# One more turned chunk per unit, and one chunk fewer on GpSimd, in a two-way state-space scan

## The chip, the cores and the metric

The kernel runs on one core of one Trainium2 chip. The metric is the device time of one execution in microseconds. A core has five engines with queues of their own: TensorE (PE), VectorE (DVE), ScalarE (ACT), GpSimd (POOL) and SyncE (SP), which here only issues DMAs. They meet at semaphores, and each works through its own instructions strictly in the order in which they are written.

## The reference, cut to what matters

There are 4 batches of 1024 tokens with 512 features. Normalisations and projections make, for each batch, `z1` and `z2` (1024 tokens by E = 1024 channels). Each goes through a state-space scan with N = 16 states per channel, the second one backward in time:

```python
dbc = einsum('bse,re->bsr', u, Wdbc)
dlt, Bm, Cm = split(dbc, [R, R + N])
delta = softplus(einsum('bsr,er->bse', dlt, Wdt) + bdt)
dA  = exp(delta[..., None] * A)                       # decay of each state
dBu = delta[..., None] * Bm[:, :, None, :] * u[..., None]   # inflow of each state
h = dA_t * h + dBu_t                                  # over the tokens t
y = einsum('ben,bn->be', h, C_t)                      # sum over the 16 states
# u * Dp is added; y1 and y2 are gated by silu(mx), added, projected by Wf,
# and gate * (projection + bf + skip) is added to x
```

## The kernel before

`setup_kernel` takes the first 0.3 ms or so: conditioning, folded weights, normalised tokens, the rows of B and C in memory. `ssm_kernel`, where the change lies, takes the rest. It is written out, without loops on the chip, as NU = 64 **units** k: batch by batch, 8 tiles of 128 channels forward, then the same 8 backward. A unit lays 128 channels on the partitions and 1024 tokens along them, and goes through 16 **chunks** c, one for each state; q = 16k + c counts chunks through. For each chunk these things happen:

- a decay: ACT takes the exponential of `delta` (line 983);
- an inflow: delta times u times the row B of this state;
- the scan itself on DVE (line 1118), with h as output;
- a product of h with the row C of this state, into one of four buffers `hbuf`;
- a sum: PE adds the product, turned, onto `y` (`sum_chunk`, line 768, 8 transposes), three steps after the scan.

The letters of the string `KINDS` say which engine does the inflow and the product:

- **V**: POOL makes the inflow (`inflow`, line 1019, into one of DR = 3 buffers `dbu`), DVE the product (line 1123).
- **P**: POOL makes both the inflow and the product (`product`, line 1024).
- **A**, a "turned" chunk: ACT scales `dut` (delta times u, turned so that tokens lie on the partitions) by a column of B, in two halves of four instructions (`scale_half`, line 945), PE turns the result back into PSUM (`turn_inflow`, line 779, 8 transposes), and POOL makes only the product.

Where the decay goes differs too. For V and P it goes into PSUM buffer `slot[q % 2]`, which is free when chunk q - 2 has been scanned (and multiplied, if that was a V). For A it goes into the single buffer `dec`, free when the A before it has been scanned; its inflow takes `slot[q % 2]`.

Each engine's order is written by hand, step by step over c. On **ACT** a step is: the decay of chunk c, then whatever the tables put there. `SCALE_STEPS` names the half of which later chunk is scaled at which step. At step 1 the second half of a sigmoid of the unit before follows (`sigmoid_half`, 4 instructions from line 920), at step 2 `copy_y` of the unit before (line 936), at steps 4 and 5 the softplus of the next unit (from line 901), and at step 15 the first half of the sigmoid. On **PE** a step c turns chunk c if it is an A, then sums chunk c - 3, then does matmul pieces for the next unit. On **POOL** a step makes the product of the chunk before (unless a V) and the inflows that `INFLOWS_AT` lists: the inflow of the third pooled chunk on, one step after its buffer is scanned.

Three sorts of units occur, by k mod 16:

- **sigmoid units** (1 to 8; 32 in all): the sigmoid halves and the matmuls `mx_part` behind them are done.
- **result units** (9 to 15 and 0, from k = 16 on; 24): at step 7 PE runs `transpose_y` for the unit before (behind the sum of chunk 4) and DVE gates it (`gate_y`, line 1092). PE projects a block of the batch before, DVE adds to it at step 1 (line 1097), and POOL finishes it (`finish_result`, lines 1030 and 1033) at step 3.
- **gating units** (9 to 15 of the first batch; 7): the same without a result block. Unit 0 has none of these.

Of the kernel before, what the change touches and what calls it, by code (L numbers as in the profile page):

```python
# [27 lines left out]
def setup_kernel(nc, t, scratch):  # L28

    with ExitStack() as ctx:  # L30
# [301 lines left out]
        def _(pe):  # L332
# [88 lines left out]
            for c in range(NC):  # L421
# [2 lines left out]
                project(1, c, ps[c % 2])  # L424


KINDS = "VPVVAVAPAVAPAPAV"
SCALE_STEPS = {0: (4, 0), 2: (4, 1), 3: (6, 0), 5: (6, 1), 6: (8, 0), 7: (8, 1),
               8: (10, 0), 9: (10, 1), 10: (12, 0), 11: (12, 1), 12: (14, 0), 13: (14, 1)}
SEQ = ET * N  # L430
HR = 4
# [5 lines left out]
def kind(q):  # L437


    return KINDS[q % N]  # L440


def before(kinds, q):

    return sum(KINDS.count(x) * (q // N) + KINDS[:q % N].count(x) for x in kinds)

# [13 lines left out]
def ssm_kernel(nc, t, scratch):  # L460

    with ExitStack() as ctx:
# [55 lines left out]
        def half(h):  # L518
            return slice(h * TC, (h + 1) * TC)
# [5 lines left out]
        def has_mx(k):  # L525
            return not gates(k) and k % (2 * ET) != 0
# [364 lines left out]
        def _(act):  # L891
# [46 lines left out]
            def scale_half(q, h):  # L938
                a, g, n = before("A", q), q // SEQ, q % N
                act.wait_ge(dut_ready, 2 * (q // N) + h + 1)  # L940
                act.wait_ge(bt_ready, g + 1)
                if a >= 2:
                    act.wait_ge(turned, a - 1)
                for j in range(TB * h, TB * h + TB):
                    last = nc.scalar.activation(abuf[:, a % 2, j * P:(j + 1) * P], dut[:, j * P:(j + 1) * P],  # L945
                                                ACT.Copy, scale=bt[:, g % 2, j, n:n + 1])
                last.then_inc(scaled, 1)
# [6 lines left out]
            def copy_dut(k, h):  # L954
                act.wait_ge(dut_mm, 2 * k + h + 1)
                if k > 0:
                    act.wait_ge(scaled, len(SCALE_STEPS) * k - 1 + h)
                nc.scalar.activation(dut[:, half(h)], mb[h][:], ACT.Copy).then_inc(dut_ready, 1)
# [9 lines left out]
            for k in range(NU):  # L968
                f, zs = wtile(k), z_step(k)
                new_b = (k + 1) % ET == 0  # L970
                for c in range(N):
# [7 lines left out]
                    else:  # L979
                        if q >= 2:  # L980
# [3 lines left out]
                                         scale=par[:, f // ET, f % ET, PA + c:PA + c + 1]).then_inc(decay_ready, 1)  # L984
                    if c in SCALE_STEPS:
                        scale_half(N * k + SCALE_STEPS[c][0], SCALE_STEPS[c][1])
                    if c == 1 and k > 0 and has_mx(k - 1):
# [220 lines left out]
```

## Time and profile before

| | us |
|---|---|
| median of 3 runs | 3499.4 |
| lowest, highest | 3492.81, 3507.31 |
| the profiled execution | 3504.69 |
| its span | 3502.9 |
| busy in the span: DVE, POOL | 3134.3, 3134.6 |
| busy in the span: PE, ACT | 2926.2, 2628.9 |

The profile holds one execution. A row of a timeline gives the start, the duration, the engine, the line, and what is written from what; in brackets stands how long the engine had been idle before and what ended that. Durations overlap a little, since an instruction's end is still being written while the next begins; so the text often takes the distance from one start to the next.

### The profile page before, as it was taken

Reading aid. Unit: us, or ns where it says so; the run is one execution under the profiler, and the core shown is the slowest. Engines: PE = TensorE matmul, PEld = TensorE weight load, DVE = VectorE, ACT = ScalarE, POOL = GpSimd, SP = SyncE. Lnnn points to the kernel's source line nnn. Section 1 sums busy time; section 2 is a strip of 40 time slices with the busy share of each in tenths; the row PEclk is TensorE's granted clock in tenths of the full one; section 3 lists DMA queues with packets and bytes.
Section 4 is the critical chain, followed back from the end, with each engine's and each line's share of the span. In section 5 each row is a group of like instructions: output and inputs, shape, how many; then the busy total and the mean of one; then the engine's idle time right before and its main releaser. Section 6 shows DMA issues by size and latency. Waiting matters only on the chain.

```text
span 3502.9 us, 47926 instructions
## 1 busy us (share of the span) xinstructions
PE 2926.2 (84%) x16208; PEld 2105.5 (60%) x16208; DVE 3134.3 (89%) x2109; ACT 2628.9 (75%) x5032; POOL 3134.6 (89%) x1418
## 2 busy tenths in 40 slices
PE   8996888887778888888888888888988888888877
PEld 4653656666656666566666666666666666666663
DVE  1853999999999999999999999999999999999970
ACT  0223888888888899887777888987777998887750
POOL 0522999999999999999999999999999999999982
PEclk9987899999899999999999999999999999999998
DMA  5566344654456344645566344645575443655444
GB/s 204 199 206 239 126 144 144 219 185 148 155 185 248 132 152 156 247 152 170 172 232 237 130 143 147 250 167 173 168 260 194 151 149 136 238 174 175 167 137 119
DMA packets 231497, 624.16 MB, mean 178 GB/s; under 512 B 22012, under 2 KB 76476, under 8 KB 227416
## 3 DMA queue, kind: packets, MB, share of 16 engines
q1 hardware_dynamic: 228520, 600.16, 49.8%
q0 software_dynamic: 2592, 18.88, 1.6%
q8 instruction: 129, 2.11, 0.2%
q10 hardware_dynamic: 144, 2.10, 0.2%
q14 instruction: 112, 0.92, 0.1%
HBM read 540.28 MB, written 80.76 MB: 177 GB/s over the span
## 4 chain that ended last, share of the span: by engine, by line
POOL 32%; issue 25%; PE 19%; DVE 14%; ACT 1%; POOLq 0%; DVEq 0%; DMA 0%; SPq 0%; ACTq 0%
POOL dbu L1019 16%; POOL hbuf L1024 15%; DVE hbuf L1118 8%; PE y L768 7%; PE mb L741 6%; DVE slot L1118 4%; PE slot L779 3%; DVE du L1068 1%; PE mb L815 1%; PE mb L818 1%; DVE delta L1058 1%; ACT abuf L945 0%; PE mb L731 0%; POOL skip L1030 0%; POOL xn L1030 0%
## 5 line engine op out<-in xcount | busy, mean ns | idle before, releaser
L1019 POOL TENSOR_TENSOR dbu<-bst,du 128x1024 f32<-128x1024 f32 x640 | 1506.6, 2373 | 37.2 <-DVE du L1068 23.7
L1024 POOL TENSOR_TENSOR hbuf<-hbuf,cres 128x1024 f32<-128x1024 f32 x640 | 1507.9, 2373 | 35.4 <-DVE hbuf L1118 34.1
L768 PE MATMUL y<-ident,hbuf 128*128 128x128 f32 x8192 | 1136.4, 290 | 292.3 <-POOL hbuf L1024 291.9
L768 PEld LDWEIGHTS y<-ident,hbuf 128*128 128x128 f32 x8192 | 1004.9, 150 | 479.3 <-POOL hbuf L1024 382.4
L945 ACT ACTIVATE abuf<-dut,bt 128x128 f32<-128x128 f32 x3072 | 971.0, 387 | 0.0
L1118 DVE TENSOR_TENSOR_SCAN hbuf<-dec,slot 128x1024 f32<-128x1024 f32 x384 | 874.5, 2277 | 38.1 <-PE slot L779 18.2
L1118 DVE TENSOR_TENSOR_SCAN slot<-slot,dbu 128x1024 f32<-128x1024 f32 x384 | 875.6, 2280 | 16.6 <-POOL dbu L1019 15.4
L983 ACT ACTIVATE slot<-delta,par 128x1024 f32<-128x1024 f32 x640 | 710.3, 1110 | 217.6 <-DVE hbuf L1123 204.9
L1118 DVE TENSOR_TENSOR_SCAN hbuf<-slot,dbu 128x1024 f32<-128x1024 f32 x256 | 580.5, 2267 | 1.2 <-ACT slot L983 1.2
L779 PE MATMUL slot<-ident,abuf 128*128 128x128 f32 x3072 | 424.8, 284 | 178.1 <-ACT abuf L945 172.4
L983 ACT ACTIVATE dec<-delta,par 128x1024 f32<-128x1024 f32 x384 | 438.3, 1141 | 153.8 <-DVE hbuf L1118 153.8
L779 PEld LDWEIGHTS slot<-ident,abuf 128*128 128x128 f32 x3072 | 362.6, 146 | 293.9 <-ACT abuf L945 203.7
L741 PE MATMUL mb<-xn,wzs 128*128 128x512 f32 x1024 | 504.6, 617 | 3.7 <-DVE delta L1058 3.7
L1123 DVE TENSOR_TENSOR hbuf<-slot,cres 128x1024 f32<-128x1024 f32 x384 | 470.2, 1224 | 13.2
L741 PEld LDWEIGHTS mb<-xn,wzs 128*128 128x128 f32 x1024 | 184.5, 201 | 140.2 <-issue 140.2
L751 PE MATMUL mb<-xn,wx 128*128 128x512 f32 x512 | 240.9, 593 | 0.0
L828 PE MATMUL mb<-wf,ybuf 128*128 128x512 f32 x448 | 207.7, 609 | 23.9 <-issue 23.9
L731 PE MATMUL mb<-dl,wdt 81*128 81x512 f32 x256 | 138.8, 656 | 47.4 <-DVE skip L1097 20.7
L828 PEld LDWEIGHTS mb<-wf,ybuf 128*128 128x128 f32 x448 | 83.5, 196 | 112.9 <-issue 112.9
L914 ACT ACTIVATE ud<-mb,par 128x512 f32<-128x512 f32 x128 | 98.3, 768 | 45.8 <-PE mb L741 45.8
L393 PE MATMUL ps<-wz,wct 128*128 128x512 f32 x256 | 121.4, 615 | 10.6 <-DMA wct<-in_wcT 10.6
L751 PEld LDWEIGHTS mb<-xn,wx 128*128 128x128 f32 x512 | 87.3, 190 | 61.2 <-issue 61.2
(101 smaller groups left out, 2050.2 us busy)
## 6 DMA issues: line engine op xcount, KB each, us to landing
bst<-bc_s SPq DMA_DIRECT2D x640, 512.0 KB, 4.2
cres<-bc_s SPq DMA_DIRECT2D x128, 512.0 KB, 8.0
wzs<-wz_s SPq DMA_DIRECT2D x64, 256.0 KB
yf_s<-yrd SPq DMA_DIRECT2D x32, 512.0 KB, 5.4
yg_s<-ybuf SPq DMA_DIRECT2D x32, 512.0 KB, 2.9
ybuf<-yf_s SPq DMA_DIRECT2D x31, 512.0 KB, 5.7
si_s<-silu SPq DMA_DIRECT2D x28, 512.0 KB, 6.1
silu<-si_s SPq DMA_DIRECT2D x28, 512.0 KB, 4.5
```

The costliest lines, as they stand in the source:

```text
L731: nc.tensor.matmul(mb[h][:], wdt[:, k % 2, :], dl[:, half(h)], start=True, stop=True).then_inc(dps_mm, 1)
L741: last = nc.tensor.matmul(mb[h][:], wz[:, k % 2, i * P:(i + 1) * P], xn[:, h, i, :], start=(i == 0), stop=(i == DT - 1))
L751: last = nc.tensor.matmul(mb[h][:], wx[:, i * P:(i + 1) * P], xn[:, h, i, :], start=(i == 0), stop=(i == DT - 1))
L768: last = nc.tensor.matmul(y[:, j * P:(j + 1) * P], hbuf[:, q % HR, j * P:(j + 1) * P], ident[:], start=False, stop=(q % N == N - 1), is_tr ...
L779: last = nc.tensor.matmul(slot[q % 2][:, j * P:(j + 1) * P], abuf[:, a % 2, j * P:(j + 1) * P], ident[:], start=True, stop=True, is_transp ...
L828: last = nc.tensor.matmul(bank[:], yp_tile(i)[:, e, :], wf[:, e, :], start=(e == 0), stop=(e == ET - 1))
L945: last = nc.scalar.activation(abuf[:, a % 2, j * P:(j + 1) * P], dut[:, j * P:(j + 1) * P], ACT.Copy, scale=bt[:, g % 2, j, n:n + 1])
L983: nc.scalar.activation(decays, delta[:, k % 2, :], ACT.Exp, scale=par[:, f // ET, f % ET, PA + c:PA + c + 1]).then_inc(decay_ready, 1)
L1019: nc.gpsimd.tensor_tensor(dbu[:, i % DR, :], bst[:, i % BR, :], du[:, k % 2, :], ALU.mult).then_inc(pool_b, 1)
L1024: nc.gpsimd.tensor_tensor(hbuf[:, q % HR, :], hbuf[:, q % HR, :], cres[:, q % N, :], ALU.mult).then_inc(pool_prod, 1)
L1118: nc.vector.tensor_tensor_scan(h[:, ::step], decays[:, ::step], inflows[:, ::step], 0.0, ALU.mult, ALU.add).then_inc(scanned, 1)
L1123: nc.vector.tensor_tensor(hbuf[:, q % HR, :], slot[q % 2][:], cres[:, c, :], ALU.mult).then_inc(dve_prod, 1)
```

## The change

Chunk 2 becomes an A (it was a V), and chunk 11 a V (it was a P). So a unit has 6 V, 3 P and 7 A, where it had 6 V, 4 P and 6 A. `SCALE_STEPS` gets two halves more, those of chunk 2 at steps 0 and 1; the halves of chunks 4 and 6 now stand at steps 2 to 5 (before: 0, 2, 3 and 5).

```diff
-KINDS = "VPVVAVAPAVAPAPAV"
-SCALE_STEPS = {0: (4, 0), 2: (4, 1), 3: (6, 0), 5: (6, 1), 6: (8, 0), 7: (8, 1),
+KINDS = "VPAVAVAPAVAVAPAV"
+SCALE_STEPS = {0: (2, 0), 1: (2, 1), 2: (4, 0), 3: (4, 1), 4: (6, 0), 5: (6, 1), 6: (8, 0), 7: (8, 1),
                8: (10, 0), 9: (10, 1), 10: (12, 0), 11: (12, 1), 12: (14, 0), 13: (14, 1)}
```

ACT's order in a sigmoid unit, from the decay of chunk 2 to that of chunk 5 (L983 is a decay, L945 x4 a scaled half, L936 `copy_y`, L901 and L903 the softplus). Before:

```order
L983 ACTIVATE slot0<-delta,par 128x1024
L945 ACTIVATE abuf<-dut,bt 128x128 x4
L936 ACTIVATE yrd<-y 128x1024
L983 ACTIVATE slot1<-delta,par 128x1024
L945 ACTIVATE abuf<-dut,bt 128x128 x4
L983 ACTIVATE dec<-delta,par 128x1024
L901 ACTIVATE soft<-mb0 128x512
L901 ACTIVATE soft<-mb1 128x512
L903 ACTIVATE soft<-soft 128x1024
L983 ACTIVATE slot1<-delta,par 128x1024
```

ACT, the same place now:

```order
L983 ACTIVATE dec<-delta,par 128x1024
L945 ACTIVATE abuf<-dut,bt 128x128 x4
L936 ACTIVATE yrd<-y 128x1024
L983 ACTIVATE slot1<-delta,par 128x1024
L945 ACTIVATE abuf<-dut,bt 128x128 x4
L983 ACTIVATE dec<-delta,par 128x1024
L945 ACTIVATE abuf<-dut,bt 128x128 x4
L901 ACTIVATE soft<-mb0 128x512
L901 ACTIVATE soft<-mb1 128x512
L903 ACTIVATE soft<-soft 128x1024
L983 ACTIVATE slot1<-delta,par 128x1024
```

The decay of chunk 2 goes to `dec`, and a scaled half stands between the decay of chunk 4 and the softplus; another half stands ahead of this piece, between the decay of chunk 1 and the sigmoid.

POOL's order from the product of chunk 13 to the product of chunk 4 of the next unit (the number in `c_in` is the product's chunk; L1019 is an inflow; in a result unit `finish_result` stands ahead of the last inflow). Before:

```order
L1024 TENSOR_TENSOR hbuf<-hbuf,cres 128x1024 [waits scanned,c_in13]
L1019 TENSOR_TENSOR dbu<-bst,du 128x1024 [waits scanned,du_ready,b_in2]
L1019 TENSOR_TENSOR dbu<-bst,du 128x1024 [waits scanned,du_ready,b_in0]
L1024 TENSOR_TENSOR hbuf<-hbuf,cres 128x1024 [waits scanned,c_in14]
L1019 TENSOR_TENSOR dbu<-bst,du 128x1024 [waits scanned,du_ready,b_in1]
L1019 TENSOR_TENSOR dbu<-bst,du 128x1024 [waits scanned,du_ready,b_in2]
L1024 TENSOR_TENSOR hbuf<-hbuf,cres 128x1024 [waits scanned,c_in1]
L1019 TENSOR_TENSOR dbu<-bst,du 128x1024 [waits scanned,du_ready,b_in0]
L1019 TENSOR_TENSOR dbu<-bst,du 128x1024 [waits scanned,du_ready,b_in1]
L1019 TENSOR_TENSOR dbu<-bst,du 128x1024 [waits scanned,du_ready,b_in2]
L1024 TENSOR_TENSOR hbuf<-hbuf,cres 128x1024 [waits scanned,c_in4]
```

POOL, the same place now:

```order
L1024 TENSOR_TENSOR hbuf<-hbuf,cres 128x1024 [waits scanned,c_in13]
L1019 TENSOR_TENSOR dbu<-bst,du 128x1024 [waits scanned,du_ready,b_in0]
L1019 TENSOR_TENSOR dbu<-bst,du 128x1024 [waits scanned,du_ready,b_in1]
L1024 TENSOR_TENSOR hbuf<-hbuf,cres 128x1024 [waits scanned,c_in14]
L1019 TENSOR_TENSOR dbu<-bst,du 128x1024 [waits scanned,du_ready,b_in2]
L1019 TENSOR_TENSOR dbu<-bst,du 128x1024 [waits scanned,du_ready,b_in0]
L1024 TENSOR_TENSOR hbuf<-hbuf,cres 128x1024 [waits scanned,c_in1]
L1019 TENSOR_TENSOR dbu<-bst,du 128x1024 [waits scanned,du_ready,b_in1]
L1024 TENSOR_TENSOR hbuf<-hbuf,cres 128x1024 [waits scanned,c_in2]
L1019 TENSOR_TENSOR dbu<-bst,du 128x1024 [waits scanned,du_ready,b_in2]
L1024 TENSOR_TENSOR hbuf<-hbuf,cres 128x1024 [waits scanned,c_in4]
```

One inflow has gone from this piece and the product of chunk 2 has come into it, so it is eleven instructions long both times. The instruction that POOL is spared is the product of chunk 11, which stood between those of chunks 10 and 12.

PE, around the start of a unit (L768 is a sum, 8 transposes each; L751 `mx_part`, L779 a turned chunk, L731 a matmul for the next unit's delta). Before:

```order
L751 MATMUL mb<-xn,wx 128x512 x2
L768 MATMUL y<-ident,hbuf 128x128 x8
L751 MATMUL mb<-xn,wx 128x512 x2
L768 MATMUL y<-ident,hbuf 128x128 x16
L731 MATMUL mb<-dl,wdt 128x512 x2
```

PE, the same place now:

```order
L751 MATMUL mb<-xn,wx 128x512 x2
L768 MATMUL y<-ident,hbuf 128x128 x8
L751 MATMUL mb<-xn,wx 128x512 x2
L768 MATMUL y<-ident,hbuf 128x128 x8
L779 MATMUL slot<-ident,abuf 128x128 x8
L768 MATMUL y<-ident,hbuf 128x128 x8
L731 MATMUL mb<-dl,wdt 128x512 x2
```

The turned chunk 2 stands between the sums of chunks 14 and 15 of the unit before.

## Rows read from the trace of the kernel before

**Rows 1.** The page's first part: each engine's busy time and share.

```profile
PE 2926.2 (84%) x16208; PEld 2105.5 (60%) x16208; DVE 3134.3 (89%) x2109; ACT 2628.9 (75%) x5032; POOL 3134.6 (89%) x1418
```

**Rows 2.** Windows: span, busy time (instructions) by engine; units 2-8, 10-14, 26-32.

```profile
core 0: us, PE busy (x) PEld busy (x) DVE busy (x) ACT busy (x) POOL busy (x), PEclk, DMA share, GB/s
422.55:753.75 331.20, 281.27 (x1606) 202.82 (x1605) 324.50 (x198) 298.33 (x569) 325.89 (x141) 0.94 0.50 172
800.68:1033.69 233.01, 177.45 (x1140) 141.76 (x1140) 231.00 (x142) 188.36 (x365) 232.79 (x101) 0.90 0.45 155
1555.26:1902.66 347.40, 292.48 (x1720) 223.43 (x1719) 328.94 (x204) 264.65 (x512) 343.74 (x155) 0.93 0.59 201
```

**Rows 3.** Waits, whole span: who waited for whom, us, times, longest.

```profile
DVE ybuf L1092 <- PE mb L818: 44.0, 32, 2.6
```

**Rows 4.** Timeline of ACT, sigmoid units 20 to 21: decay 15 to decay 5.

```profile
1312.03 1.12 ACT L983 ACTIVATE slot<-delta,par 128x1024 f32<-128x1024 f32 x1 [0.43 <-DVE hbuf L1118]
1315.09 0.69 ACT L920 ACTIVATE soft<-mb,par 128x512 f32<-128x512 f32 x1 [1.94 <-PE mb L751]
...
1317.67 1.10 ACT L983 ACTIVATE slot<-delta,par 128x1024 f32<-128x1024 f32 x1
1318.71 1.26 ACT L945 ACTIVATE abuf<-dut,bt 128x128 f32<-128x128 f32 x4
1319.88 1.10 ACT L983 ACTIVATE slot<-delta,par 128x1024 f32<-128x1024 f32 x1
...
1332.21 1.12 ACT L983 ACTIVATE slot<-delta,par 128x1024 f32<-128x1024 f32 x1 [0.22 <-DVE hbuf L1123]
```

**Rows 5.** Timeline of DVE there: scans 14 and 15, later scan 5, scan 14.

```profile
1312.55 2.29 DVE L1118 TENSOR_TENSOR_SCAN hbuf<-dec,slot 128x1024 f32<-128x1024 f32 x1 [0.55 <-issue]
1314.76 2.27 DVE L1118 TENSOR_TENSOR_SCAN slot<-slot,dbu 128x1024 f32<-128x1024 f32 x1
1317.06 1.23 DVE L1123 TENSOR_TENSOR hbuf<-slot,cres 128x1024 f32<-128x1024 f32 x1
1318.20 0.74 DVE L1078 SCALAR_TENSOR_TENSOR silu<-mb,par,soft 128x512 f32<-128x512 f32 x1
...
1334.29 2.27 DVE L1118 TENSOR_TENSOR_SCAN slot<-slot,dbu 128x1024 f32<-128x1024 f32 x1
...
1359.61 2.29 DVE L1118 TENSOR_TENSOR_SCAN hbuf<-dec,slot 128x1024 f32<-128x1024 f32 x1 [0.55 <-issue]
```

**Rows 6.** Timeline of PE, end of unit 21: sum 10, turn 14, sum 11, `mx_part`.

```profile
1355.40 1.09 PE L768 MATMUL y<-ident,hbuf 128*128 128x128 f32 x8 [1.27 <-POOL hbuf L1024]
...
1358.48 1.04 PE L779 MATMUL slot<-ident,abuf 128*128 128x128 f32 x8
1359.35 1.04 PE L768 MATMUL y<-ident,hbuf 128*128 128x128 f32 x8
1360.23 1.88 PE L751 MATMUL mb<-xn,wx 128*128 128x512 f32 x4
```

**Rows 7.** Timeline of POOL, result units 28 to 29: products 12 and 13, product 4.

```profile
1696.42 4.71 POOL L1024 TENSOR_TENSOR hbuf<-hbuf,cres 128x1024 f32<-128x1024 f32 x2 [0.30 <-DVE hbuf L1118]
...
1724.58 2.36 POOL L1024 TENSOR_TENSOR hbuf<-hbuf,cres 128x1024 f32<-128x1024 f32 x1
```

**Rows 8.** Timeline of PE, result unit 29: the sum of chunk 4.

```profile
1726.99 1.97 PE L768 MATMUL y<-ident,hbuf 128*128 128x128 f32 x8 [3.36 <-POOL hbuf L1024]
```

**Rows 9.** Timeline of DVE, result units 28, 29: gating, scans 8, 13 and 15.

```profile
1680.84 0.69 DVE L1092 TENSOR_TENSOR ybuf<-mb,silu 128x512 f32<-128x512 f32 x1 [1.84 <-PE mb L818]
...
1683.33 2.29 DVE L1118 TENSOR_TENSOR_SCAN hbuf<-dec,slot 128x1024 f32<-128x1024 f32 x1 [0.24 <-PE slot L779]
...
1730.49 1.49 DVE L1092 TENSOR_TENSOR ybuf<-mb,silu 128x512 f32<-128x512 f32 x2 [1.36 <-PE mb L818]
1732.22 2.29 DVE L1118 TENSOR_TENSOR_SCAN hbuf<-dec,slot 128x1024 f32<-128x1024 f32 x1 [0.24 <-PE slot L779]
...
1745.08 2.27 DVE L1118 TENSOR_TENSOR_SCAN hbuf<-slot,dbu 128x1024 f32<-128x1024 f32 x1
...
1750.10 2.27 DVE L1118 TENSOR_TENSOR_SCAN slot<-slot,dbu 128x1024 f32<-128x1024 f32 x1
```

## The prediction

> **What bounds the kernel now.** I read the busy shares first, then windows cut at unit borders, then the waits, then timelines of two places. The page shows DVE and POOL level at 89% [rows 1], which tells nothing of which waits for which, so I went by sorts of units [rows 2]. Seven sigmoid units take 331.2 us, 47.3 each, with DVE busy 324.5 and POOL 325.9; five gating units 46.6 each, DVE and POOL both within 0.5 us of full; seven result units 49.6 each, POOL busy 343.7 of 347.4, but DVE only 328.9, so DVE is idle 2.6 us in each. The waits name where: DVE waits for `transpose_y` at the gating [rows 3].
>
> In a sigmoid unit the reader should see that DVE sets the pace. Scan 14 begins at 1312.55 and again at 1359.61: 47.06 us, of which 0.55 is a wait at scan 14 [rows 5]; DVE's own work is thus 46.5. PE makes that wait: at step 13 its sum had waited 1.27 us for POOL, and the matmuls behind it stood ahead of the turning of chunk 14 [rows 6].
>
> In a result unit I see a loop through three engines. POOL starts products 12 and 13 as soon as scan 12 lets it [0.30 idle, rows 7], works without a pause to product 4 of the next unit, and PE had waited 3.36 us for that product [rows 8]; the sum and the transposes end DVE's wait at the gating, 1.36 us [rows 9]; from there DVE runs to scan 13, and the loop closes. One turn, 1680.84 to 1730.49, is 49.65 us [rows 9].
>
> **The change part by part.** What it removes: one POOL instruction per unit. Product 13 starts near 1696.42 + 2.33 = 1698.75 and product 4 ends at 1726.94, 28.2 us for eleven instructions and a finished block [rows 7]; a POOL instruction is about 2.33 (two products in 4.67, from 1696.42 to 1701.1). So POOL is spared 2.33 x 64 = 149 us. But the one it is spared, product 11, stands outside the stretch from product 13 to product 4, and that stretch keeps eleven instructions. DVE does the same sixteen scans and six products; one product moves from chunk 2 to chunk 11. One broadcast of B fewer per unit leaves SP's queue; none of the waits I read ends on one, so I cost it at nothing.
>
> What it adds: on PE 8 transposes, 0.87 us at the upper clock (1358.48 to 1359.35 [rows 6]), between the sums of chunks 14 and 15; behind them queue sum 15, and behind that `copy_y` on ACT. On ACT two scaled halves, 1.17 each (1318.71 to 1319.88 [rows 4]), 2.34 us per unit.
>
> **Sigmoid units.** Before, ACT's run from the sigmoid at 1315.09 has no listed wait until decay 5, where it waits 0.22 [rows 4]. Decay 5 ends at 1332.21 + 1.12 = 1333.33, and scan 5 starts at 1334.29 [rows 5]: 0.96 to spare, 1.18 with the wait. Now five halves stand ahead of decay 5, where three did: 2.34 later. And DVE comes to scan 5 earlier: chunk 2 as a V took 2.30 + 1.14 = 3.44, as an A 2.21 (1312.55 to 1314.76), so 1.23 [rows 5]. If ACT's run starts where it did, DVE waits 2.34 + 1.23 - 1.18 = 2.4 us at scans 3 to 5.
>
> It can start earlier. Before, it stood 1.94 us waiting for `mx_part` and began 0.33 after scan 15 (1315.09 against 1314.76). With POOL relieved, PE need not be late at step 13. The turning of chunk 14, sum 11 and `mx_part` take 0.87 + 0.88 + 1.88 = 3.6 us [rows 6] from the end of scan 12, two scans or 4.4 us ahead of scan 15, with 0.1 for the hand-over: 0.7 ahead of scan 15 at best. I take 0.5 ahead, 0.83 earlier, and a wait of 1.6. The bound is ACT's own decay 15, ending at 1312.03 + 1.04 = 1313.07, which is 1.14 ahead of an undelayed scan 15 (1314.76 - 0.55): wait 0.9. So the wait is 0.9 to 2.4, taken 1.6. The old 0.55 goes, since PE comes in time at scan 14. A sigmoid unit becomes 46.5 + 1.6 = 48.1, 1.0 longer; 28 units (2 to 8 of each batch) give +28. Four units (9, 25, 41, 57) start behind the last sigmoid unit and have no 0.55 to regain: +6. For the four first sigmoid units I put +3 in all, a guess between nothing and 1.6 each.
>
> **Result units.** DVE's way from scan 8 to the end of scan 13 was 1745.08 + 2.27 - 1732.22 = 15.13 [rows 9]; with chunk 11 as a V it is 1.23 longer, 16.36. Product 13 follows scan 13 by about 0.2, since product 12 (2.33) starts with the end of scan 12 and a scan takes 2.2. Then the 28.2 of POOL. From 1726.94 to the gating at 1730.49 is 3.55, and from there to scan 8 it was 1.73 in one unit and 2.49 in the other. Sum: 16.36 + 0.2 + 28.2 + 3.55 + 1.73 = 50.0, with 2.49 50.8; the mean of before was 49.6. I take +0.9 for each of the 20 long ones: +18. The range is -1.1 (below) to +1.5. ACT's two halves come late here too, but that wait at scan 5 only shortens the one at the gating, which is 1.36 and more.
>
> **Gating units and unit 16** have no finish (2.6 us less on POOL), so they run at DVE's pace: the ACT wait shows there, without the sigmoids, and no row gives it. Bounds are 0 and the 1.6 of above; I take 0.8 x 7 = +6.
>
> **Sum.** 28 + 6 + 3 + 18 + 6 = +61. The profiled execution took 3504.7 (span 3502.9 and 1.8 around it), 5 above the median of 3499.4. So 3566 against its own time, 3560 against the median.
>
> **The rivals.** First, the other side: **POOL's relief passes through.** The Trainium skill (Perfetto Trace Analysis, "Identifying the Most-Contended Engine") takes, for Vector, Scalar and GpSimd, the engine with the highest occupancy as the one to relieve first. By that rule a shorter POOL shortens the kernel. As a mechanism here: POOL's lateness makes PE late [rows 6, 8] and PE makes DVE wait; if product 4 came 2.3 us earlier, result units would shed up to 2.3 x 24 = 55 us, and sigmoid units up to 0.8 x 32 = 26. That gives about 3420. It decides if the wait on product 4 is POOL's total load and not its order; for it speaks POOL's 343.7 of 347.4 [rows 2], against it that the eleven instructions stay eleven and start from scan 13. Chance 0.09.
>
> Second, **the covers hold.** ACT starts at its bound (wait 0.9, sigmoid units +0.35 x 28 = +10, with the four behind them +4), and PE runs at its upper level at the gating. The 8 transposes of sum 4 took 1.97 after 3.36 us of idling [rows 8] and take 1.04 when PE has been running [rows 6]: the lower and the upper of the two levels, 1.2 and 2.4 GHz. At the upper level sum 4 and a first half of 8 transposes take 0.87 x 2 and some 0.3 of hand-over, 2.0 for 3.55; the loop is 48.5, -1.1 x 20 = -22. With +9 for the rest: about 3500, no change. The added transposes shorten PE's idle stretch, which speaks for it; PE still waits for product 4 each time, which speaks against. The Trainium skill (TensorE: Matmul & The Clock Gate, "HAM oscillation") says that gaps in PE's work bring the clock back down and each burst then starts cold; the trace agrees in the 1.97 against 1.04. Chance 0.13.
>
> Third, **both bounds at their dear end**: sigmoid units +1.9 x 32, result units +1.5 x 24, the others +1.6 x 7: +108, 3607. For it speaks that ACT and PE work strictly in order, so one late piece delays what is behind. Chance 0.10.
>
> **How the numbers follow.** The forecast, +20 to +95 with 3560 as its centre, has 0.68; with the third rival slower has 0.78. The measurement can tell about 0.5%, 17 us, from no change. Slower by over 0.5%: 0.78; within: 0.13; faster: 0.09. The range 3515 to 3605 leaves out the first rival, most of the second and the top of the third, about 2 in 10.
>
> **What would show it.** Right: POOL's busy time falls by about 150 us while the span grows; DVE waits for ACT at line 1118 at the start of sigmoid units (scans 3 and 5, 1 to 2.4 us, new); DVE's wait for PE at line 1092 stays or grows above 44 us; sigmoid units near 48.1, result units near 50 to 51. Wrong: result units at 48.5 or less, or no wait of scans for decays; then the relief of POOL counts for more than I think.

## The result and the profile after

The changed kernel took 3597.6 us (median of 4 runs, 3596.6 to 3606.8), the kernel before 3503.1 beside it: a ratio of 1.0278, with an interval from 1.0254 to 1.0302. It is slower by 94 us. The forecast was 3560, its range 3515 to 3605. The profiled execution of after took 3606.8, 102.1 more than that of before; the working below is about these 102.

The page of after begins with each engine's busy time and share, as [rows 1] does:

```profile
PE 3014.6 (84%) x16720; PEld 2185.3 (61%) x16720; DVE 3143.9 (87%) x2109; ACT 2782.1 (77%) x5544; POOL 2988.2 (83%) x1354
```

POOL works 146 us less, and the span is 102 us longer. DVE's work is the same within 10 us, so what came is waiting. The windows of units 2 to 8, 10 to 14 and 26 to 32, as [rows 2], tell in which sorts of units:

```profile
core 0: us, PE busy (x) PEld busy (x) DVE busy (x) ACT busy (x) POOL busy (x), PEclk, DMA share, GB/s
423.53:763.46 339.93, 288.34 (x1661) 212.15 (x1660) 325.40 (x197) 314.80 (x625) 309.75 (x134) 0.94 0.44 157
812.83:1061.74 248.91, 190.47 (x1180) 154.15 (x1180) 231.98 (x141) 200.75 (x405) 221.36 (x96) 0.88 0.38 135
1601.38:1958.76 357.38, 301.04 (x1772) 227.22 (x1771) 329.69 (x204) 281.32 (x568) 327.14 (x148) 0.93 0.54 185
```

Seven sigmoid units take 48.6 us each (47.3 before), five gating units 49.8 (46.6), seven result units 51.1 (49.6). The largest step, 3.2 us, is in the gating units, whose POOL is now idle for a tenth of the time. Of the waits, these four bear on the units (engine, line, whom it waited for, us in all, times, longest):

```profile
POOL hbuf L1024 <- DVE hbuf L1118: 281.4, 121, 4.2
...
DVE slot L1118 <- ACT slot L983: 79.3, 101, 1.4
DVE ybuf L1092 <- PE mb L818: 50.9, 38, 2.1
DVE hbuf L1118 <- PE slot L779: 40.4, 34, 7.8
```

The first stood at 34.1 us before, the second at 1.0, the fourth at 18.2; the third answers to [rows 3]. What POOL was relieved of it spends waiting for DVE.

**A result unit.** The timeline of after from unit 27 to 28, as [rows 7 to 9] (start, duration, engine, line, operation; idle before and its releaser in brackets): POOL's products 12 and 13 of unit 27, its product 4 and its products 12 and 13 of unit 28, PE's sum 4, DVE's gating, scan 8 and scan 13.

```profile
1694.62 4.71 POOL L1024 TENSOR_TENSOR hbuf<-hbuf,cres 128x1024 f32<-128x1024 f32 x2 [3.92 <-DVE hbuf L1118]
...
1722.79 2.36 POOL L1024 TENSOR_TENSOR hbuf<-hbuf,cres 128x1024 f32<-128x1024 f32 x1
...
1745.73 4.71 POOL L1024 TENSOR_TENSOR hbuf<-hbuf,cres 128x1024 f32<-128x1024 f32 x2 [3.93 <-DVE hbuf L1118]
...
1725.20 1.97 PE L768 MATMUL y<-ident,hbuf 128*128 128x128 f32 x8 [4.26 <-POOL hbuf L1024]
...
1728.98 0.69 DVE L1092 TENSOR_TENSOR ybuf<-mb,silu 128x512 f32<-128x512 f32 x1 [2.10 <-PE mb L818]
1730.43 0.69 DVE L1092 TENSOR_TENSOR ybuf<-mb,silu 128x512 f32<-128x512 f32 x1 [0.76 <-PE mb L818]
1731.36 2.29 DVE L1118 TENSOR_TENSOR_SCAN hbuf<-dec,slot 128x1024 f32<-128x1024 f32 x1 [0.24 <-PE slot L779]
...
1745.51 2.27 DVE L1118 TENSOR_TENSOR_SCAN hbuf<-slot,dbu 128x1024 f32<-128x1024 f32 x1
```

This is the loop of the prediction with its own terms. Scan 8 to the end of scan 13: 1745.51 + 2.27 - 1731.36 = 16.42. Product 13 follows 0.28 later, since product 12 (2.33) began at 1745.73. Product 13 of unit 27 began at 1694.62 + 2.33 = 1696.95, and product 4 ends at 1722.79 + 2.36 = 1725.15: 28.20. From there to the first gating 3.83, and to scan 8 another 2.38. Sum 51.1. POOL waits for scan 12 in each of the long result units (1.9 to 4.2 us, 3.9 in most), where before it waited 0.3 in every second one. The time that it was spared is of no use to it: product 4 comes the same 28.2 us after product 13.

**A sigmoid unit.** Timeline of after, units 20 to 21, as [rows 4, 5]: ACT's sigmoid and decay 5, DVE's scan 15 and scans 3 and 5.

```profile
1304.50 0.69 ACT L920 ACTIVATE soft<-mb,par 128x512 f32<-128x512 f32 x1 [0.65 <-PE mb L751]
...
1324.03 1.10 ACT L983 ACTIVATE slot<-delta,par 128x1024 f32<-128x1024 f32 x1
...
1304.79 2.27 DVE L1118 TENSOR_TENSOR_SCAN slot<-slot,dbu 128x1024 f32<-128x1024 f32 x1
...
1318.70 2.30 DVE L1118 TENSOR_TENSOR_SCAN slot<-slot,dbu 128x1024 f32<-128x1024 f32 x1 [1.19 <-ACT slot L983]
...
1325.17 2.30 DVE L1118 TENSOR_TENSOR_SCAN slot<-slot,dbu 128x1024 f32<-128x1024 f32 x1 [0.71 <-ACT slot L983]
```

ACT's run starts 0.29 ahead of scan 15 and DVE waits at scans 3 and 5 for the two decays, 1.9 us here.

**A gating unit.** Here the prediction had no row. Timeline of after, the border to unit 14: POOL's product 14 of unit 13; PE's sum 14, the turning of chunk 2 (L779), sum 15; ACT's `copy_y` and decay 3; DVE's scans 2 and 3.

```profile
1012.68 2.36 POOL L1024 TENSOR_TENSOR hbuf<-hbuf,cres 128x1024 f32<-128x1024 f32 x1
...
1015.09 1.97 PE L768 MATMUL y<-ident,hbuf 128*128 128x128 f32 x8 [5.84 <-POOL hbuf L1024]
1016.86 1.91 PE L779 MATMUL slot<-ident,abuf 128*128 128x128 f32 x8
1018.56 1.79 PE L768 MATMUL y<-ident,hbuf 128*128 128x128 f32 x8
...
1020.39 1.02 ACT L936 ACTIVATE yrd<-y 128x1024 f32<-128x1024 f32 x1 [4.09 <-PE y L768]
1021.31 1.11 ACT L983 ACTIVATE slot<-delta,par 128x1024 f32<-128x1024 f32 x1
...
1018.86 2.29 DVE L1118 TENSOR_TENSOR_SCAN hbuf<-dec,slot 128x1024 f32<-128x1024 f32 x1 [1.47 <-PE slot L779]
1022.46 2.30 DVE L1118 TENSOR_TENSOR_SCAN slot<-slot,dbu 128x1024 f32<-128x1024 f32 x1 [1.31 <-ACT slot L983]
```

The same place in the trace of before: sums 14 and 15 in one run, `copy_y`, decay 3, scan 3.

```profile
990.68 3.67 PE L768 MATMUL y<-ident,hbuf 128*128 128x128 f32 x16 [5.83 <-POOL hbuf L1024]
...
994.39 1.02 ACT L936 ACTIVATE yrd<-y 128x1024 f32<-128x1024 f32 x1 [1.36 <-PE y L768]
995.32 1.11 ACT L983 ACTIVATE slot<-delta,par 128x1024 f32<-128x1024 f32 x1
...
996.51 2.29 DVE L1118 TENSOR_TENSOR_SCAN slot<-slot,dbu 128x1024 f32<-128x1024 f32 x1
```

Before, decay 3 ended at 995.32 + 1.11 = 996.43, and scan 3 began at 996.51: this chain had 0.08 us to spare. It starts with product 14, which stands on POOL behind inflows 0 and 1 of the next unit. Now the turning of chunk 2 lies inside the chain, 1.70 from start to start, since PE comes out of 5.8 us of idling at its lower level (granted clock 0.52 of full speed from 1015.09 to 1020.30; before, 0.50 from 990.68 to 994.30); and DVE reaches scan 3 by 1.23 sooner. 1.70 + 1.23 - 0.08 = 2.85, and the two waits sum to 2.78. A third, 0.71 at scan 5, follows.

### The profile page after: what moved, and what is told of

It reads as the page before. It is cut to its first block, busy times and chain, and to the rows that moved or that the text cites. A ratio compares the mean times of both kernels' runs of the same rounds, so it can differ in the third digit from the quotient of the medians.

```text
span 3605.3 us, 49462 instructions
## 1 busy us (share of the span) xinstructions
PE 3014.6 (84%) x16720; PEld 2185.3 (61%) x16720; DVE 3143.9 (87%) x2109; ACT 2782.1 (77%) x5544; POOL 2988.2 (83%) x1354
## 4 chain that ended last, share of the span: by engine, by line
PE 38%; POOL 19%; issue 12%; ACT 11%; DVE 10%; SPq 1%; DMA 0%; POOLq 0%; DVEq 0%; ACTq 0%
PE y L768 14%; POOL hbuf L1024 12%; PE mb L741 8%; PE slot L779 8%; POOL dbu L1019 6%; DVE hbuf L1118 5%; ACT abuf L945 5%; PE mb L828 4%; DVE slot L1118 3%; ACT slot L983 2%; ACT dec L983 2%; DVE du L1068 2%; ACT soft L901 2%; PE mb L815 1%; DVE delta L1058 1%
## 5 line engine op out<-in xcount | busy, mean ns | idle before, releaser
L1024 POOL TENSOR_TENSOR hbuf<-hbuf,cres 128x1024 f32<-128x1024 f32 x640 | 1512.5, 2373 | 281.4 <-DVE hbuf L1118 281.4
L768 PE MATMUL y<-ident,hbuf 128*128 128x128 f32 x8192 | 1164.8, 291 | 434.8 <-POOL hbuf L1024 433.7
L768 PEld LDWEIGHTS y<-ident,hbuf 128*128 128x128 f32 x8192 | 1008.1, 150 | 642.8 <-POOL hbuf L1024 546.6
L1019 POOL TENSOR_TENSOR dbu<-bst,du 128x1024 f32<-128x1024 f32 x576 | 1362.0, 2376 | 38.3 <-DVE du L1068 22.0
L945 ACT ACTIVATE abuf<-dut,bt 128x128 f32<-128x128 f32 x3584 | 1132.8, 387 | 0.0
L1118 DVE TENSOR_TENSOR_SCAN hbuf<-dec,slot 128x1024 f32<-128x1024 f32 x448 | 1019.6, 2276 | 53.0 <-PE slot L779 40.4
L983 ACT ACTIVATE slot<-delta,par 128x1024 f32<-128x1024 f32 x576 | 638.8, 1109 | 153.2 <-DVE hbuf L1123 109.0
L983 ACT ACTIVATE dec<-delta,par 128x1024 f32<-128x1024 f32 x448 | 511.3, 1141 | 140.9 <-DVE hbuf L1118 140.7
L779 PE MATMUL slot<-ident,abuf 128*128 128x128 f32 x3584 | 528.9, 296 | 79.5 <-ACT abuf L945 52.9
L779 PEld LDWEIGHTS slot<-ident,abuf 128*128 128x128 f32 x3584 | 453.3, 153 | 196.7 <-ACT abuf L945 113.0
L1118 DVE TENSOR_TENSOR_SCAN hbuf<-slot,dbu 128x1024 f32<-128x1024 f32 x192 | 435.6, 2269 | 0.0
L751 PE MATMUL mb<-xn,wx 128*128 128x512 f32 x512 | 240.9, 593 | 0.0
L731 PE MATMUL mb<-dl,wdt 81*128 81x512 f32 x256 | 129.8, 630 | 17.9 <-DMA dl<-bc_s 8.6
L936 ACT ACTIVATE yrd<-y 128x1024 f32<-128x1024 f32 x64 | 65.3, 1021 | 88.2 <-PE y L768 88.2
L751 PEld LDWEIGHTS mb<-xn,wx 128*128 128x128 f32 x512 | 87.3, 190 | 61.2 <-issue 61.2
```

Of the source, the lines that this page charges most:

```text
L731: nc.tensor.matmul(mb[h][:], wdt[:, k % 2, :], dl[:, half(h)], start=True, stop=True).then_inc(dps_mm, 1)
L751: last = nc.tensor.matmul(mb[h][:], wx[:, i * P:(i + 1) * P], xn[:, h, i, :], start=(i == 0), stop=(i == DT - 1))
L768: last = nc.tensor.matmul(y[:, j * P:(j + 1) * P], hbuf[:, q % HR, j * P:(j + 1) * P], ident[:], start=False, stop=(q % N == N - 1), is_tr ...
L779: last = nc.tensor.matmul(slot[q % 2][:, j * P:(j + 1) * P], abuf[:, a % 2, j * P:(j + 1) * P], ident[:], start=True, stop=True, is_transp ...
L983: nc.scalar.activation(decays, delta[:, k % 2, :], ACT.Exp, scale=par[:, f // ET, f % ET, PA + c:PA + c + 1]).then_inc(decay_ready, 1)
L1019: nc.gpsimd.tensor_tensor(dbu[:, i % DR, :], bst[:, i % BR, :], du[:, k % 2, :], ALU.mult).then_inc(pool_b, 1)
```

## The experiments

Lengths of units are mean distances between the starts of scan 0 on DVE's timeline of one profiled execution: sigmoid units 2 to 8 of each batch (28), gating units 10 to 15 (6), long result units 26 to 32, 42 to 48 and 58 to 62 (19). All in us; each ratio is to the kernel before as it ran on the same chip beside it (medians 3496.0 for e1 to e4, 3503.8 for e5 to e11, 3500.8 for f1 to f4). Since these differ by up to 8 us, kernels of different groups are compared by their ratios; 0.1% is 3.5 us.

| kernel | median | ratio to before [interval] | sigmoid | gating | result |
|---|---|---|---|---|---|
| before | 3503.1 | | 47.28 | 46.73 | 49.64 |
| after | 3597.6 | 1.0278 [1.0254, 1.0302] | 48.72 | 49.86 | 50.86 |
| e1, result block late | 3550.2 | 1.0148 [1.0124, 1.0171] | 48.61 | 49.85 | 48.78 |
| e2, chunk 2 turned alone | 3536.3 | 1.0101 [1.0076, 1.0127] | 48.18 | 47.96 | 49.43 |
| e3, chunk 11 a V alone | 3555.3 | 1.0164 [1.0139, 1.0188] | 47.83 | 47.73 | 50.92 |
| e4, chunk 2's halves cheap | 3583.1 | 1.0244 [1.0219, 1.0268] | 48.12 | 49.87 | 50.97 |
| e5, inflow 1 late | 3575.8 | 1.0208 [1.0181, 1.0234] | 48.20 | 48.34 | 51.00 |
| e6, `copy_y` late | 3588.6 | 1.0242 [1.0213, 1.0271] | 48.63 | 48.04 | 51.07 |
| e10, softplus split | 3569.2 | 1.0198 [1.0172, 1.0223] | 47.76 | 48.91 | 51.05 |
| e11, those four together | 3571.6 | 1.0199 [1.0178, 1.0220] | 49.81 | 47.18 | 48.96 |
| f1, three of them | 3501.4 | 1.0007 [0.9994, 1.0021] | 47.44 | 47.91 | 48.82 |
| f2, before, result block late | 3487.8 | 0.9967 [0.9951, 0.9983] | 47.27 | 46.73 | 49.19 |
| f3, e2 with three moves | 3489.9 | 0.9972 [0.9958, 0.9986] | 47.44 | 46.54 | 49.15 |
| f4, pattern by unit | 3490.2 | 0.9962 [0.9945, 0.9978] | 47.22 | 46.72 | 48.90 |

### The two halves of the change

e2 is after with chunk 11 left a P; e3 is before with chunk 11 a V.

```diff
 e2: -KINDS = "VPAVAVAPAVAVAPAV"     e3: -KINDS = "VPVVAVAPAVAPAPAV"
     +KINDS = "VPAVAVAPAVAPAPAV"         +KINDS = "VPVVAVAPAVAVAPAV"
```

> Half the change: chunk 2 is an A as in the changed kernel (two more halves on ACT, 8 more transposes on PE), but chunk 11 stays a P, so a unit has 5 V, 4 P, 7 A; DVE has one product less than in either kernel (1.2 us per unit), POOL as many instructions as before. Theory: sigmoid units keep the waits for ACT at scans 3 and 5 (about 1.9 us) but DVE's work is 45.3, so about 47.2 (before 47.3); result units have DVE's short way from gating to scan 13 again, 15.1 us, and come back to 49.6; gating units keep their waits, about 48.7. Total within 15 us of the kernel before, 3500 to 3515. Rival (ACT's load alone makes the loss): result and gating units stay near the changed kernel's 51.2 and 49.9, total 3570 or more.

> The other half: chunk 11 is a V as in the changed kernel, chunk 2 stays a V, so a unit has 7 V, 3 P, 6 A; POOL has one product less, DVE one product more (1.2 us per unit), ACT and PE as before. Theory: result units get the longer way from gating to scan 13 and go to 50.6 to 51.2 (before 49.6); sigmoid units have no new wait for ACT: DVE's work 47.7 and little else, 47.7 to 48; gating units 47.7. Total +35 to +50 on before, about 3545. Rival (POOL's total load makes the result units' wait): with 2.3 us less on POOL result units fall below 49.6, to 48.5, total 3510 or less.

In e3 the units come as expected within 0.03 us; the total is 59 us over before, where 35 to 50 was expected. Its result units take what after's take (50.92), so the V at chunk 11 alone makes their loss. e2 gives the result units back (49.43), but sigmoid units stay at 48.18 where 47.2 was expected, and the time is 3536, not 3500 to 3515. I had taken a DVE that has a product less for a unit that is that much shorter; it only comes earlier to the same decays, and waits 0.79 and 0.72 us at scans 3 and 5. The two halves nearly sum to the whole: 1.01% and 1.64% against 2.78%. In the sigmoid units they do (0.90 + 0.55 against 1.44), in the gating units not (1.23 + 1.00 against 3.13).

### Is the result units' loop what the prediction says?

e1 moves the finishing of the result block out of the stretch from product 13 to product 4, and the store of the block, on SP, behind it:

```diff
-                    if c == 6 and block_before is not None:     # SP: store_result
+                    if c == 9 and block_before is not None:
-                    if c == 3 and k > 0 and projection_of(k - 1) is not None:    # POOL: finish_result
+                    if c == 6 and k > 0 and projection_of(k - 1) is not None:
```

> The changed kernel with POOL's two instructions of finish_result moved from step 3 to step 6, behind the product of chunk 4, and SP's store of that block from step 6 to step 9. No other work changes. Theory (order): a result unit is a loop of POOL's stretch from product 13 to product 4, PE's sum and transposes, and DVE from the gating to scan 13; the finish, 2.6 us, leaves that stretch, so DVE's wait at the gating (2.1 and 0.8 us) nearly goes and the 20 long result units fall from 51.2 us to 48.5 to 49, by 2.2 to 2.7 each: 45 to 55 us less than the changed kernel, about 3547. Sigmoid and gating units stay. Rival (load of ACT): the result units are long because ACT's two added halves delay decays; then moving POOL's finish changes nothing, 3597. Second rival (PE's clock): the wait at the gating is slow transposes; then about a third of it goes, 3580.

It came as forecast: 3550 (1.30% less than after, some 46 us), result units 48.78. The view of line 1092 in e1 lists what DVE still waited there:

```profile
its engine sat idle before it (us, times) until:
  PE mb L818: 1.3, 1
```

50.9 us have become 1.3, with 2.6 us less in the stretch and POOL's work the same (2986.6 us busy, 2988.2 in after). So the loop through product 4 set the result units, in its order and not in its load.

### Which wait costs what in the other units

e4 scales chunk 2 in two instructions instead of eight (each half by the column of B of its first 128 tokens, so the inflow of this chunk is another).

> The changed kernel with each of chunk 2's two scaled halves done by one instruction of 512 columns instead of four of 128 (one column of B for the whole half, so chunk 2's inflow is not the reference's). ACT loses about 0.68 us per half, both ahead of decays 3 and 5; nothing else moves. Theory (ACT's order): sigmoid units' wait at scan 3 falls by up to 1.4 us and the units from 48.6 to 47.6 to 47.9, 28 units: 20 to 28 us less than the changed kernel; gating and result units stay, since there ACT waits for PE or DVE for POOL. About 3573. Rival (PE's chain: product 14, sum 14, turn 2, sum 15, copy_y holds ACT in sigmoid units too): under 10 us less.

Sigmoid units fall by 0.60, where 0.7 to 1.0 was expected, and the total by 0.34%, some 12 us, where 20 to 28 was expected and under 10 by the rival. So it lies between the two: the wait at scan 3 falls from 0.92 to 0.38 us and does not go, and the one at scan 5 stays (0.68). Gating units do not move (49.87 against 49.86). The length of ACT's two halves is thus a price in the sigmoid units and not in the gating units. What binds the gating units is tried by e5 and e6. e5 lets product 14 go ahead of the next unit's inflow 1 on POOL; e6 puts `copy_y` behind decay 3 on ACT; e10 puts the softplus's exponential behind decay 5.

```diff
 e5, inflow_step:
-    return max(POOLED[i - DR] + 1, POOLED[i] // N * N - 2)
+    return max(POOLED[i - DR] + 1, POOLED[i] // N * N - 2 + (POOLED[i] % N == 1))
 e6, ACT:
-                    if c == 2 and k > 0:
+                    if c == 3 and k > 0:
                         copy_y(k - 1)
 e10, ACT: the two lines of the exponential (902, 903) go from the softplus's first part,
           step 4, to the head of its last part, step 5
```

> The changed kernel with one thing moved on POOL: the inflow of the next unit's chunk 1 stands behind the product of chunk 14 instead of ahead of it, so that product ends 2.3 us earlier. No work is added or taken away. Theory (PE's chain in units without sigmoid): product 14 releases sum 14, behind which PE's turning of chunk 2, sum 15 and so ACT's copy_y and decay 3 queue; gating units lose the 1.4 us wait for the turning at scan 2 and most of the 1.1 us at scan 3, 49.9 to 47.3 to 48; sigmoid units lose only copy_y's 0.3 us, 48.7 to 48.4; result units stay at 50.9, being held by product 4. Together 7 units by 2 to 2.5 and 28 by 0.3: about 22 us less than the changed kernel, 3575. Rival (the waits in gating units are ACT's load): no change, 3597.

> The changed kernel with copy_y on ACT moved from step 2 to step 3, so behind decay 3 instead of ahead of it. Theory: in sigmoid units ACT runs without a pause from its sigmoid to decay 5, so only the order changes: scan 3's wait of 0.9 goes and scan 5's grows by as much, units stay at 48.4 to 48.7; in gating units ACT stood 4 us waiting in copy_y, so decay 3 comes in time and units fall by about 1.0. Total 5 to 15 us less, about 3587. Rival (copy_y alone is what decay 3 is late by): sigmoid units fall by 0.9 to 47.8, total 30 us less, 3565.

> The changed kernel with the softplus's exponential (1.06 us) moved on ACT from step 4 to step 5, so behind decay 5 and its scaled half instead of ahead. Theory (ACT's order up to decay 5 sets sigmoid units): decay 5 comes 1.06 us earlier, the wait of 0.7 at scan 5 goes in sigmoid and gating units, 0.6 to 0.7 each, 36 units: about 25 us less than the changed kernel, 3573; result units stay at 50.9, their wait at scan 5 being hidden in that at the gating. Rival: delta, made on DVE right behind the product of chunk 5, is then late by as much; no change.

e5 comes near its forecast in total (3576 for 3575). It takes 1.52 us from a gating unit, where 1.9 to 2.6 was expected, and ends the wait at scan 2. Its timeline at the border to unit 14 (PE's sum 14 and turned chunk 2, DVE's scans 2 and 3):

```profile
1003.16 1.97 PE L768 MATMUL y<-ident,hbuf 128*128 128x128 f32 x8 [3.52 <-POOL hbuf L1024]
1005.73 1.94 PE L779 MATMUL slot<-ident,abuf 128*128 128x128 f32 x8 [0.60 <-DVE hbuf L1123]
...
1007.76 2.29 DVE L1118 TENSOR_TENSOR_SCAN hbuf<-dec,slot 128x1024 f32<-128x1024 f32 x1
1011.48 2.30 DVE L1118 TENSOR_TENSOR_SCAN slot<-slot,dbu 128x1024 f32<-128x1024 f32 x1 [1.43 <-ACT slot L983]
```

The turning of chunk 2 now waits for nothing of POOL but for DVE: it writes `slot[0]`, and chunk 0, a V, holds that buffer until its product is made. Sum 15, `copy_y` and decay 3 are behind it still, and so 1.43 us at scan 3 remain here (1.04 in the mean gating unit). e10 gives its forecast total (3569 for 3573), with the wait at scan 5 gone; 0.96 is off a sigmoid unit, where 0.6 to 0.7 was expected. e6 gives the forecast total too (3588.6 for 3587), but not by the way I gave: in sigmoid units the waits at scans 3 and 5 are both gone, and one of 1.72 us for PE stands at scan 4 in their place; gating units fall by 1.82, where about 1.0 was expected.

### The four moves together

> The changed kernel with all four moves of order: POOL's finish at step 6, the inflow of chunk 1 behind product 14, copy_y behind decay 3, the softplus's exponential behind decay 5. The work is that of the changed kernel. Theory (orders, not loads, cost the time): result units near DVE's own 47.2, 47.3 to 48; sigmoid units 47.3 to 47.8 (some ACT lateness before decay 5 stays, 0.5 to 1); gating units 46.6 to 47.3. That is 3465 to 3490, faster than the kernel before by 0.3 to 1%. Rival (ACT is full: 45 us of work in 46.5): sigmoid units stay at 48.5, total 3520.

This failed: 3571.6 where 3465 to 3490 was expected, and 3520 by the rival, with sigmoid units of 49.8, longer than after's. The timeline of e11 at the start of sigmoid unit 20 (PE's skip terms at line 761, which overwrite `y`, and its turned chunk 4; ACT's `copy_y`; DVE's scan 4):

```profile
1308.52 1.94 PE L761 MATMUL y<-ident,ud 128*128 128x128 f32 x8 [3.10 <-ACT yrd L936]
...
1311.65 1.04 PE L779 MATMUL slot<-ident,abuf 128*128 128x128 f32 x8
...
1307.38 1.00 ACT L936 ACTIVATE yrd<-y 128x1024 f32<-128x1024 f32 x1
...
1312.78 2.29 DVE L1118 TENSOR_TENSOR_SCAN hbuf<-dec,slot 128x1024 f32<-128x1024 f32 x1 [2.90 <-PE slot L779]
```

PE may write `y` anew only when ACT has copied it. A later `copy_y` holds up the skip terms, behind which sum 0 and the turning of chunk 4 queue, and PE idles 3.1 us and comes back at its lower level (1.94 for 8 transposes). The move had been meant to clear decay 3, which it does; its price is of the same sort as in e6, and larger. The same unit in e6:

```profile
1299.95 1.06 PE L761 MATMUL y<-ident,ud 128*128 128x128 f32 x8 [2.70 <-ACT yrd L936]
...
1301.72 1.04 PE L779 MATMUL slot<-ident,abuf 128*128 128x128 f32 x8
...
1302.85 2.29 DVE L1118 TENSOR_TENSOR_SCAN hbuf<-dec,slot 128x1024 f32<-128x1024 f32 x1 [1.56 <-PE slot L779]
```

There PE comes back at its upper level (granted clock 1.00, here 0.53). From the start of the skip terms to that of the turning it takes 1.77 us there and 3.13 here, and these 1.36 us are the 1.34 by which DVE waits longer. In e6, 20 of the 28 sigmoid units are like this one, with 0.7 to 1.6 us at scan 4; in e11 all 28 wait 2.85 us or more. Why PE idles longer in e11 (3.1 to 3.5 us, in e6 2.7 at most) was not tried.

### Without that move, and on the kernel before

f1 is e11 without the move of `copy_y`. f2 is before with e1's edit alone, f3 is e2's letters with f1's three moves. f4 gives the letters of after, inflow 1 late and the split softplus to units 26 to 32, 41 to 48 and 57 to 63 alone, the letters and steps of before to all others, and the late result block to all (the lines that choose the letters; those on steps and counts left out as ...):

```diff
-KINDS = "VPVVAVAPAVAPAPAV"
+KINDS_BY = ("VPVVAVAPAVAPAPAV", "VPAVAVAPAVAVAPAV")
...
+def late_turn(k):
+    return 1 if k > 2 * ET and (k - 1) % (2 * ET) >= ET and k > 3 * ET + 1 else 0
...
-    return KINDS[q % N]
+    return KINDS_BY[late_turn(q // N)][q % N]
```

(The texts on f1 and f2 speak of DVE at step 9; what stands there is SP's store. DVE's addition stays at step 1. Of the softplus, f1 moves the exponential alone; the logarithm stays where it was.)

> The changed kernel with three of its orders moved at once: the result block is finished on POOL behind the inflows of step 6 and added on DVE at step 9, inflow 1 of a unit comes one step later on POOL (so product 14 of the unit before comes ahead of it), and the softplus's exponential and logarithm come one step later on ACT (behind the decay of the chunk after). The copy of y stays at step 2. Theory: each move ends one of the three waits by itself (result units 48.8 when moved alone, gating units 48.3, sigmoid units 47.8), and they concern different waits, so they add up: sigmoid units 47.3 to 47.6, gating units 47.2 to 47.8, result units 48.0 to 48.8, about 3475 to 3495 us against 3500. Rival: as with the copy of y, a move only hands the wait to the next engine in line; then the time stays at 3540 or more.

> The kernel before with the one move that shortened the result units of the changed kernel: the result block finished on POOL behind the inflows of step 6, added on DVE at step 9. Theory: with four products of pooled chunks POOL's own work in a result unit is 343.7 / 7 = 49.1 us, so moving the block out of the stretch from product 13 to product 4 cannot take a result unit (49.6) under 49.1: about -10 us, 3485 to 3497. Rival: the stretch is what counts whatever POOL's total is; then result units go to 48.8 or less as in the changed kernel, -1 us or more x 20, 3480 or less.

> Chunk 2 turned and chunk 11 left as POOL's own (five V, four P, seven A), with the three moves (result block late, inflow 1 one step later, softplus split). DVE has one product less per unit (1.14 us), POOL keeps its four. Theory: the pace is then set by POOL (46.5 in a sigmoid unit, 49.1 in a result unit) and by ACT's run from the sigmoid to decay 5; with the latter relieved, sigmoid units 46.8 to 47.4, gating units 46.8 to 47.3, result units 49.1 to 49.4: 3475 to 3500. Rival: the waits of DVE for ACT at scans 3 and 5 stay, since DVE comes earlier still; sigmoid units 48 or more, 3520 or more.

> The patterns of both kernels in one: the units with a result block (26 to 32, 42 to 48, 58 to 63 and the unit ahead of the later ones) have the changed letters, with inflow 1 late and the softplus split; all other units have the letters and steps of the kernel before. The result block is finished late in all. Theory: POOL's spared product is worth something only where POOL has the finish besides, so result units take 48.0 to 48.8 (49.6 before) and the others what they took before: 20 x -0.9 to -1.5 = -18 to -30 us, 3470 to 3485. Rival: the borders between the two patterns cost (a decay in the wrong buffer, a half scaled too late), or gains are handed to the sigmoid units: 3495 or more.

f1 is back at the time of before (1.0007), 96 us under after: three moves, none of which takes away any work, undo the change's whole loss. Sigmoid units are 47.44 as forecast; gating units 47.91, a little over, with the 1.43 of e5 left at scan 3. The total missed its window by 6 us. In result units (48.82, as e1) a wait shows at scan 10 that after did not have (1.25 us on average; 0.52 in e1). The rows are of unit 28: POOL's finish ahead of product 6, PE's sum 6 and turned chunk 10, DVE's scan 10:

```profile
1681.96 1.29 POOL L1030 TENSOR_TENSOR skip<-skip,gateb 128x512 f32<-128x512 f32 x1
...
1684.57 4.67 POOL L1024 TENSOR_TENSOR hbuf<-hbuf,cres 128x1024 f32<-128x1024 f32 x2
...
1686.97 1.09 PE L768 MATMUL y<-ident,hbuf 128*128 128x128 f32 x8 [2.65 <-POOL hbuf L1024]
...
1689.62 1.04 PE L779 MATMUL slot<-ident,abuf 128*128 128x128 f32 x8
...
1690.75 2.29 DVE L1118 TENSOR_TENSOR_SCAN hbuf<-dec,slot 128x1024 f32<-128x1024 f32 x1 [0.71 <-PE slot L779]
```

The finish, moved, makes product 6 late, and that PE. f2 came as forecast: result units 49.19, against a floor of 49.1 from POOL's own work. Its window of units 26 to 32, in the columns of the windows above:

```profile
1538.40:1882.49 344.09, 293.18 (x1715) 215.83 (x1714) 328.18 (x205) 265.85 (x512) 342.86 (x155) 0.95 0.61 203
```

POOL is busy 342.9 of 344.1 us: there its load is the bound, as it was not in after. f3 lies in its window too (sigmoid units 0.04 over theirs, gating units 0.3 under). f4's result units (48.90) gained 0.74 each against before, not 0.9 to 1.5, and it missed its window by 5 us. f2, f3 and f4 are 0.3 to 0.4% faster than before, less than the 0.5% that I had named as what can be told; their intervals exclude no change all the same, and from the first scan to the last f2, f3 and f4 are 12.8, 5.4 and 13.9 us shorter than before in the traces. Which of the three is best, these runs can't tell. But f1, f3 and f4 all have the late result block, and none of them is faster than before with that one move (f2, 3487.8; f1 takes 14 us more): in no order tried did the changed letters themselves gain time.

## Why the prediction was right, and where not

**The sign and, in the result and sigmoid units, the mechanism** were right; the size was too small, +61 us for the 94 measured, and the gating units were misread. POOL's busy time fell by 146 us (149 worked out) while the span grew; the stretch from product 13 to product 4 kept its length, 28.2 and 28.20.

**Result units**: each term of the sum came within 0.3 us, and the last lies between its two values: 16.42 for 16.36, 0.28 for 0.2, 28.20 for 28.2, 3.83 for 3.55, 2.38 for 1.73 to 2.49. The mean unit is 50.86, +1.22, where I took +0.9; with unit 63, 23 us for 18.

**Sigmoid units**: the waits at scans 3 and 5 sum to 1.63 us on average (1.6 taken). The unit is 48.72 all the same, not 48.1: another 0.25 stands at scan 2, which waits for the added turning (a price that I had put at nothing). The prediction let the 0.55 at scan 14 of one unit stand for all; the mean unit of before waited 0.40 at scan 8 and 0.29 at scan 14, and of these 0.13 at scan 8 are left. That is 1.63 + 0.25 - 0.56 = 1.32 of the 1.44; the other 0.12 lies in small waits that I did not follow. The start of ACT's run, 0.29 ahead of scan 15, lies between the 0.5 taken and the dear bound. 28 units cost 40 us for 28, the four behind them 8 for 6, the four first ones 8 for 3; in those the wait at scan 8 for PE grew as well (3.13 for 2.35).

**Gating units and unit 16** are the step that failed. I wrote that no row gives their price and bounded it by 0 and 1.6; they cost 3.1 each, 22 us for 6. The rows were there, in the trace of before: the sums at 990.68, decay 3 and scan 3, with 0.08 us to spare. I had costed the added transposes at the upper level (0.87, taken from a busy stretch) and named what queues behind them, but not asked how late that already was where PE comes out of a long wait. The three waits there average 1.41 at scan 2, 1.13 at scan 3 and 0.71 at scan 5. Here e4 (gating units unmoved) excludes the length of ACT's halves. e5 confirms the chain through product 14 for 1.52 of the 3.13 us, and e6 and e10 take 1.82 and 0.95 by moves behind it; f1 still has 1.18 over before.

**Sum**: 40 + 8 + 8 + 23 + 22, with 2 for unit 0 and -3 ahead of it, is 100; behind the last scan another 2 come, which gives the 102 of the profiles. Of the 41 more than the +61 forecast, 16 are the gating units and 12 the long run of sigmoid units.

**The rivals.** POOL's relief did not pass through: its idle time went to line 1024, from 34.1 to 281.4 us. The rule of the Trainium skill (Perfetto Trace Analysis, "Identifying the Most-Contended Engine"), to relieve the engine with the highest occupancy first, would by itself have pointed the wrong way here: POOL went from 89 to 83% and the kernel lost 94 us. It is no clean trial of the rule, since DVE stood level with POOL and the change adds to ACT and PE. The covers didn't hold: sum 4 took 1.97 after 4.26 us of idling, as before after 3.36. The third rival's total (3607) is nearer than my forecast, though not its parts: result units fell short of its dear end (23 for 36 us), sigmoid units too (48 for 61), gating units passed it (22 for 11).

## What to carry to other kernels

Taking work from the busiest engine helps only if the work stood in the stretch that others wait for; ask from which instruction to which the loop runs, and count what stands between. For an instruction that is added to a queue, look up the slack of whatever queues behind it at the place with the least slack, in each sort of stage, and cost it at the clock level found there. And a move that ends one wait can start another two engines on (`copy_y` and the skip terms), and can cost more beside other moves than alone: read the row of the new wait in the single run before putting moves together.

## What the runs showed that I had not expected

- The turning of chunk 2 can start no earlier than DVE's product of chunk 0, since both use `slot[0]` (e5: 0.60 us of PE's idling ends on it). The sum ahead of it follows on 3.52 us of idling, and the turning then takes 1.94 us and sum 15 behind it 1.91: PE is at its lower level (granted clock 0.50 from 1003.16 to 1009.60).
- The set-up, the same code in all kernels, is not equally long from one execution to the next: the first scan began at 316.2 us in the profile of before, at 302.4 in that of f2, 313.4 in that of after. For differences of 10 us the distance from the first scan to the last tells more than the span of a single profile; why the set-up varies was not tried.
